# Row sums and inverse deviations of a graph layer's joint stage move to a PSUM bank of their own, and the transposed weighted rows of two edge groups share one bank

## What the reference computes

```
h = relu(layernorm(x))                       # each row on its own: mean and variance over 64 features
score = sum(h[src] * h[dst]); a = softmax of score over the edges with one dst
out = segment_sum((h @ W_conv + b)[src] * a, dst) + relu(h @ W_res + b)
x = x + batchnorm(out)                       # mean and variance over all 100000 rows
h2 = relu(layernorm(x))
x = h2 + gelu(gelu([h2, boxes] @ W_c1 + b) @ W_c2 + b), plus x
    where boxes = segment_sum(gelu(gelu([h2[dst'], h2[src'], edge] @ W_m1) @ W_m2), index)
```

## Time and profile before

| what | value |
|---|---|
| time, median of three runs (range) | 1961.68 us (1946.9 to 1965.65) |
| span of the profiled execution, first to last instruction | 1753.3 us |
| median of the runs less that span | 208.4 us |
| PE busy / DVE busy / ACT busy / POOL busy | 1375.6 / 1361.7 / 833.2 / 1363.7 us |
| mean granted TensorE clock | 0.831 |

### The profile page before, as it was taken

The page is one execution under the profiler, slowest core; times in us unless marked ns, Lnnn a source line. Parts: engine busy times, 40 slices in busy tenths (PEclk is TensorE's granted clock), DMA queues, the critical chain, the costliest instruction groups (busy, mean ns, idle before and its releaser), DMA issues.

```text
span 1753.3 us, 21724 instructions
## 1 busy us (share of the span) xinstructions
PE 1375.6 (78%) x6521; PEld 942.1 (54%) x6521; DVE 1361.7 (78%) x2229; ACT 833.2 (48%) x1448; POOL 1363.7 (78%) x1135
## 2 busy tenths in 40 slices
PE   3487777777776776988999889858889988787993
PEld 1266666666555564766667666634445444343541
DVE  8899899989877858898889888825767766555871
ACT  4655455545543435776668666621333432332441
POOL 7777777778777778788888887675767768888676
PEclk9788889888887877898889888955888987886987
DMA  7788776545543363444545565545656554545520
GB/s 210 249 283 290 282 264 219 165 145 157 161 150 96 106 224 102 157 166 166 201 162 186 174 200 178 160 98 108 121 120 124 118 117 97 107 89 98 122 48 18
DMA packets 154342, 273.55 MB, mean 156 GB/s; under 512 B 58386, under 2 KB 69361, under 8 KB 154228
## 3 DMA queue, kind: packets, MB, share of 16 engines
q1 hardware_dynamic: 71144, 183.91, 31.1%
q0 software_dynamic: 68112, 49.85, 16.7%
q10 hardware_dynamic: 14972, 38.41, 5.9%
HBM read 151.68 MB, written 121.80 MB: 156 GB/s over the span
## 4 chain that ended last, share of the span: by engine, by line
POOL 40%; issue 20%; DVE 18%; PE 13%; DMA 6%; ACT 2%; SPq 0%; POOLq 0%; DVEq 0%; ACTq 0%
POOL agg_rows L591 11%; POOL out L591 10%; POOL agg_ring L587 7%; DVE stat L756 4%; POOL xt L637 3%; DVE stat L764 3%; POOL part L587 3%; DMA rr<-edge_x 3%; DMA edge_agg<-agg_ring 2%; POOL rr L631 2%; DVE xc L770 1%; PE banks L1350 1%; DVE sums L821 1%; PE banks L1542 1%; PE banks L1540 1%
## 5 line engine op out<-in xcount | busy, mean ns | idle before, releaser
L587 POOL DMA_INDIRECT agg_ring<-agg_rows,edge_idx x196 | 233.2, 1190 | 112.2 <-DMA edge_agg<-agg_ring 57.2
L591 POOL DMA_INDIRECT agg_rows<-agg,put_first x196 | 234.0, 1194 | 55.9 <-issue 54.7
L587 POOL DMA_INDIRECT part<-in_x,edge_idx x192 | 217.3, 1132 | 58.5 <-issue 58.2
L591 POOL DMA_INDIRECT out<-agg,put_last x196 | 212.0, 1082 | 59.6 <-issue 59.6
L1335 PE MATMUL banks<-ident,xc 128*128 128x128 f32 (+1 forms) x784 | 135.1, 322 | 141.6 <-DVE xc L770 140.9
L1466 PEld LDWEIGHTS banks<-packed,cT 97*128 97x128 f32 (+1 forms) x1568 | 210.4, 218 | 45.3 <-issue 44.3
L1466 PE MATMUL banks<-packed,cT 97*128 97x64 f32 (+1 forms) x1568 | 218.6, 303 | 0.5 <-ACT cT L1198 0.5
L1335 PEld LDWEIGHTS banks<-ident,xc 128*128 128x128 f32 (+1 forms) x784 | 113.3, 177 | 152.0 <-DVE xc L770 130.8
L1456 PE MATMUL banks<-hT,packed 64*96 64x512 f32 (+1 forms) x392 | 125.5, 718 | 47.6 <-ACT cT L1198 43.0
L1081 ACT ACTIVATE hT<-banks 128x512 f32<-128x512 f32 (+1 forms) x98 | 55.4, 595 | 205.7 <-PE banks L1335 204.3
L587 POOL DMA_INDIRECT x_ring<-in_x,edge_idx x104 | 121.4, 1167 | 34.2 <-issue 34.2
(11 more groups left out here) (163 smaller groups left out, 3351.2 us busy)
## 6 DMA issues: line engine op xcount, KB each, us to landing
xt<-in_x SPq DMA_DIRECT2D x84, 512.0 KB, 5.2
r_rows<-rT ACTq DMA_DIRECT2D x48, 512.0 KB, 5.4
agg_rows<-rb SPq DMA_DIRECT2D x48, 512.0 KB
out<-xt SPq DMA_DIRECT2D x36, 512.0 KB, 3.0
edge_r<-rr ACTq DMA_DIRECT2D x48, 256.0 KB, 5.0
rT<-r_rows SPq DMA_DIRECT2D x24, 512.0 KB, 6.5
part<-r_rows SPq DMA_DIRECT2D x24, 512.0 KB, 6.9
rr<-edge_r SPq DMA_DIRECT2D x48, 256.0 KB, 3.2
```

Of the source, the lines that this page charges most:

```text
L587: A.indirect_dma_start(to, None, table[:, :], bass.IndirectOffsetOnAxis(ap=idx, axis=0), bounds_check=limit, oob_is_err=False).then_inc(si ...
L591: A.indirect_dma_start(table[:, :], bass.IndirectOffsetOnAxis(ap=idx, axis=0), rows_of, None, bounds_check=limit, oob_is_err=False).then_i ...
```

## The change

Bank 5 of PSUM becomes `row_stat`. The row sums of `center` and `edge_center` are written there by L764, and L766 reads them there. The last instruction of the inverse deviations (L702) writes its result there instead of to `stat`, and `relu_scale` (L770) reads it there. Since bank 5 is taken, the transposed weighted rows of even and odd groups both go to bank 4: `transpose_weighted(n)` waits for the scan of group n-1 instead of n-2, and TensorE's order changes: only the transposes of a-2 stand at the head of a round, those of b-2 come after `conv_product(a-2)`.

```diff
--- before.py
+++ after.py
@@ -217,6 +217,7 @@
             return W[i // 2][:, (i % 2) * HALF:(i % 2 + 1) * HALF]
 
         bank_sum = bank(3)
+        row_stat = bank(5)
 
         s_w = sem("weights_loaded")
         s_idx = sem("edge_idx_loaded")
@@ -689,7 +690,7 @@
         def _(dve):
             V = nc.vector
 
-            def inverse_sqrt(total, tmp, n_mean, eps, done):
+            def inverse_sqrt(total, tmp, n_mean, eps, done, root=None):
                 v, y, a = tmp
                 done(V.tensor_scalar(v, total, n_mean * SQUEEZE, eps * SQUEEZE, ALU.mult, ALU.add))
                 done(V.tensor_scalar(y.bitcast(I32), v.bitcast(I32), -0.5, MAGIC, ALU.mult, ALU.add))
@@ -699,7 +700,8 @@
                 done(V.tensor_tensor(a, y, y, ALU.mult))
                 done(V.tensor_tensor(a, a, v, ALU.mult))
                 done(V.scalar_tensor_tensor(out=a, in0=a, scalar=-CUBIC1, in1=a, op0=ALU.add, op1=ALU.mult))
-                done(V.scalar_tensor_tensor(out=y, in0=a, scalar=CUBIC0, in1=y, op0=ALU.add, op1=ALU.mult))
+                done(V.scalar_tensor_tensor(out=y if root is None else root, in0=a, scalar=CUBIC0, in1=y, op0=ALU.add,
+                                            op1=ALU.mult))
 
             def in_stage(st, step):
                 k = [0]
@@ -777,6 +779,12 @@
                 return stat[0:p, i, 2 * R + (g % 2) * ER:2 * R + (g % 2 + 1) * ER]
 
 
+            def node_stat(i, s, p):
+                return row_stat[0:p, i * P + (s % 2) * R:i * P + (s % 2 + 1) * R]
+
+            def edge_stat(i, n, p):
+                return row_stat[0:p, i * P + 2 * R + (n % 2) * ER:i * P + 2 * R + (n % 2 + 1) * ER]
+
             dve.wait_ge(s_m, 1)
 
             def center(s):
@@ -784,19 +792,19 @@
                 dve.wait_ge(A_x.of(s), A_x.after(s))
                 A_t.done(dve, s - CS)
                 A_sq.done(dve, s - 2)
-                subtract_mean(xc[s % CS][0:p, :], xt[s % XS][0:p, :], dstat(0, s, p), A_ctr, s, 1)
+                subtract_mean(xc[s % CS][0:p, :], xt[s % XS][0:p, :], node_stat(0, s, p), A_ctr, s, 1)
 
             def edge_center(n):
                 p = edges_of(group_of(n))
                 dve.wait_ge(G_x.of(n), G_x.after(n))
                 E_t.done(dve, n - 4)
                 E_w.done(dve, n - 4)
-                subtract_mean(ec[n % 4][0:p, :], x_ring[n % GS][0:p, :], estat(0, n, p), E_ctr, n, 1)
+                subtract_mean(ec[n % 4][0:p, :], x_ring[n % GS][0:p, :], edge_stat(0, n, p), E_ctr, n, 1)
 
             def edge_score(n):
                 p = edges_of(group_of(n))
                 t_ = ec[n % 4][0:p, :]
-                relu_scale(rows(t_), rows(t_), estat(3, n, p), E_h)
+                relu_scale(rows(t_), rows(t_), edge_stat(1, n, p), E_h)
                 dve.wait_ge(E_h.sem, E_h.after(n))
                 E_sc.done(dve, n - 1)
                 V.tensor_tensor(rows(prod[0:p, :]), side(t_, 0), side(t_, 1), ALU.mult).then_inc(E_sc.sem, 1)
@@ -819,7 +827,7 @@
                 E_scan.done(dve, n - 1)
                 carry = sums[1 - n % 2][:, 0:1] if n else 0.0
                 V.tensor_tensor_scan(sums[n % 2][:, 0:c][:, ::-1], same[n % 2][0:D + 1, 0:c][:, ::-1],
-                                     bank(4 + n % 2)[0:D + 1, 0:c][:, ::-1], carry,
+                                     bank(4)[0:D + 1, 0:c][:, ::-1], carry,
                                      ALU.mult, ALU.add).then_inc(E_scan.sem, 1)
 
             def edge_finish(n):
@@ -839,7 +847,7 @@
                 A_ss.done(dve, last_step)
                 E_ss.done(dve, last_edge)
                 inverse_sqrt(stat[:, 1, c0:c1], tuple(stat[:, i, c0:c1] for i in (2, 3, 4)), 1.0 / D, LN_EPS,
-                             in_stage(N_inv, t_))
+                             in_stage(N_inv, t_), row_stat[:, P + c0:P + c1])
 
             for t_ in range(ROUNDS):
                 steps = node_pair(t_)
@@ -872,7 +880,7 @@
                     if s is not None:
                         p = nodes_of(s)
                         h_ = rows(xc[s % CS][0:p, :])
-                        relu_scale(h_, h_, dstat(3, s, p), A_h)
+                        relu_scale(h_, h_, node_stat(1, s, p), A_h)
                     if is_group(n):
                         edge_score(n)
                     if is_group(n - 2):
@@ -1353,9 +1361,9 @@
             def transpose_weighted(n):
                 p = edges_of(group_of(n))
                 pe.wait_ge(E_w.sem, E_w.after(n))
-                E_scan.done(pe, n - 2)
+                E_scan.done(pe, n - 1)
                 for j in range(EJ):
-                    ins = T.transpose(bank(4 + n % 2)[0:D + 1, j:p * EJ:EJ], weighted[n % 2][0:p, j, :],
+                    ins = T.transpose(bank(4)[0:D + 1, j:p * EJ:EJ], weighted[n % 2][0:p, j, :],
                                       ident[0:p, 0:p])
                 ins.then_inc(E_wt.sem, 1)
 
@@ -1403,9 +1411,8 @@
             for t_ in range(ROUNDS):
                 steps = node_pair(t_)
                 edges = edge_pair(t_)
-                for n in edges:
-                    if is_group(n - 2):
-                        transpose_weighted(n - 2)
+                if is_group(edges[0] - 2):
+                    transpose_weighted(edges[0] - 2)
                 for n in edges:
                     if is_group(n - 4):
                         edge_stats(n - 4)
@@ -1420,6 +1427,8 @@
                         edge_r_product(n)
                     if is_group(n - 2):
                         conv_product(n - 2)
+                    if n == edges[0] and is_group(n - 1):
+                        transpose_weighted(n - 1)
 
 
             pe.wait_ge(s_bnd, BN_PARTS)
```

## The result

The changed kernel takes 2089.68 us (median of four runs, 2074.5 to 2100.1), the kernel before, run beside it, 1954.29 us (1942.1 to 1965.7): ratio 1.066, 95% interval 1.057 to 1.074. That is 135 us slower, where 43 us were forecast, and outside the range. The sign and the place were right; the size was not, and the trace from which it was worked out turned out not to be one of the timed executions.

What follows compares the result with a forecast made beforehand. VectorE was taken to bound the joint stage, then late gathers. New wait 74.1, gather waits -28.9, node stage -1.9 and PSUM operands 0 gave +43.3 us, from 1961.7 to 2005.0 us; range 1986 to 2038.

Steps and rivals of the forecast that it cites:

- The sign and the place: Slower by over 1% (chance 0.92), through a new VectorE wait before each round's second scan.
- the sum: Whole kernel: new wait 74.1, gather waits -28.9, node stage -1.9, PSUM operands 0, together +43.3 us.
- The new wait: Joint stage, second scan of a round: VectorE waits for TensorE's late transposes, mean 3.50 us per full round, 74.1 in all.
- The waits for gathers: Joint stage, row sums from group 37 on: five VectorE waits for gathered rows disappear, -28.9 us.
- much slower: Rival, TensorE's chain: clock stays low to its end, 2077 us, about 2040 in half the rounds; chance 0.14.
- The operands in PSUM: VectorE's 13 instructions per full round using the new bank: -1.6 to +4.6 us by the rows, taken as 0.
- The 21 us: Same VectorE instructions: estimate from the skill page's 65 ns more per PSUM access, not adopted in the forecast.
- The port rival: GpSimd's gathers shorten, order doesn't count: 1930.9 us, if the new wait is under 1.3 us per round; chance 0.03.
- No change: Rival, TensorE's chain: clock stays high, each full round waits only 1.24 us, 1962.1 us (+0.4); chance 0.05.

Runs made afterwards that it cites:

- e6: Kernel before the change, unedited, run again with its own profile: 1740.4 us.
- e16: Kernel before the change, unedited, run later for its trace: 1970.9 us, one execution.
- e5: Changed kernel, unedited, beside the kernel before: 1777.3 us against 1740.8, ratio 1.021.
- e7: Changed kernel, unedited, once more: 1792.2 us in a single execution, beside 1745.5 for the kernel before.
- e17: Changed kernel, unedited, run later for its trace: 2076.5 us, one execution.
- e1: Kernel before with only TensorE's new order; sums and deviations stay in SBUF, a bank for each group parity: 1782.27 us against 1741.24, ratio 1.024.
- e3: Changed kernel with the transposes of b-2 moved up, right behind the transposes of group a: 1724.51 us, ratio 0.990 to the kernel before.
- e4: Kernel before with the transposes of b-2 at e3's early place; sums and deviations in SBUF, separate banks: 1743.92 us, ratio 1.001.
- e11: Kernel before with 64 added transposes in front of the first step's transposes in each round: 1873.3 us.
- e12: Changed kernel with the same 64 added transposes per round as e11: 1957.5 us.
- e18: Same kernel as e3, unedited, run later for its trace: 2022.7 us, one execution.
- e15: Kernel before with TensorE's idle time before the first step's transposes filled by 24 identity transposes: 1996.2 us, beside 1962.4 without.

## Why the prediction was wrong, point by point

**The failed step** is the last of the sum: "The profiled span of 1753.3 would become 1796.6; with the 208.4 us that lie between span and median in the table, unchanged, 1961.7 + 43.3 = 2005.0 us." The spans lie only about 2 us under their times. The 208.4 us were the difference between an execution of the first level and timed runs of the second, and they lay inside the joint stage, in waits of VectorE (231.6 of the 235 us between e6 and e16), largely behind the engine whose chain was being priced. The sum priced the first level: +43.3, measured +36.5 (e5) and +46.7 (e7, one execution). At the second level two of its terms are wrong. The new wait, 74.1 us, measured 295.1 us (226.5 + 68.6). The waits for gathers, -28.9 us, aren't there to be saved: e16 has none. The kernel before has other waits there, 287.7 us in all (e16), and a part of them goes when the new wait comes: the changed kernel has 387.6 us in all (e17). The difference, +99.9 us, is nearly the whole of the +105.6 us between these two executions.

**The new wait.** Right in place and mechanism: e1 alone 82.3 us, e5 78.6, and e3 takes it away. The chain was sized from a trace of the first level. The rival "much slower" (2040 to 2077, chance 0.14) asked for TensorE's clock to stay at its lower level to the end of the chain. That came true in half of the rounds: in the changed kernel's first profile the conv product of group a-2 runs at 0.50 from start to end in 12 of 25 rounds, in the profile of before and in e5 in none. Its price was about right as well (2.4 us of work more in the round shown above, where it had 2.8). But the same chain is 5.1 us longer by idle time, behind signals of TensorE that come late, and for this no rival had a place. So the rival is the nearest to the measured 2089.7 us in part by luck. Whether the low clock comes from the idle time, or both from one cause, stays open.

**The gathers.** Their waits are gone, as forecast, in e5 and in e1. In e1 82.3 us of new waits cost 41 us; 28.9 of the other 41 would be these waits, and for the remaining 12 no run names a place. At the second level the kernel before has no such waits, and the term is nothing.

**The operands in PSUM.** At 0 ns for VectorE the term held: 682 and 691 ns against 676 and 692. The 21 us by the Trainium skill, page "VectorE: DVE Perf Modes", section on the TRN2 errata, did not appear. The port rival was half true: the gathers got shorter, and once the new wait is taken out the kernel with the operands in PSUM is 19 us faster (e3 against e4). The shorter gathers are as the Trainium skill, page "SBUF — State Buffer", section "Who interferes with whom", would have it. The rival lost against the order, by the condition given for it: a new wait of under 1.3 us per round, where 3.3 were measured.

**No change.** The clock would have had to stay high in the chain; it did not (1.97 us for the eight transposes above, as in the earlier trace rows).

**What of the 135 us is shown.** 36 to 47 us are the order at the first level. The delay by hand shows that a late TensorE costs the changed order more, up to 84 us, since the old one has room. The rest was seen and not explained: at the second level ScalarE's copies start late for 290 us in the changed kernel and for 143 us in the kernel before (e17, e16), and the chain runs more often at the lower clock. The second level gave +106 us in e17 against e16 and +135 us in the first comparison, so its size is known to some 30 us only. Why TensorE's signals come late there, and why more often in the changed kernel, stays open.

## What to carry to other kernels

Before pricing a change, put the profiled span beside the time of its own execution; if only a median of other runs is given and it is far from the span, the trace may be of another condition, and the missing time can sit in the chain that the change touches. A step moved behind a chain costs that chain's lateness as well as its length: of TensorE's first delay the old order passed on 46 to 51 us, the changed one 81 to 96. An idle time without a named cause is best checked against the end of what the program makes it wait for. And split a change that does two things: at the first level the PSUM operands, shared bank included, were a gain of 19 us, the late place of four transposes a loss of 53 (e5 against e3), and only the place had to differ.

## What the runs showed of the hardware that was not expected

- The same kernel took 1741 us at some times and 1962 us at others, with all executions made together at one level. The whole difference was in one stage. The record numbers the chips, and chip 6 stands beside both: 1741.0 us with e11 and e12, 1965.9 us with e16 half an hour later. So the number of the chip doesn't settle the level.
- At the second level what follows TensorE starts late by up to 14 us, and once in each of e16, e17 and e18 by 38 to 49 us, after TensorE's work has ended by the record; at the first level never by over 0.32 us. In e15 TensorE is also seen to stop between matmuls that wait for nothing: in the rows above they start 0.73 to 2.10 us apart, with the granted clock at 0.54 over the stretch and DMA at a share of 0.26:

```profile
553.00:569.40 16.40, 5.51 (x15) 2.68 (x15) 10.79 (x14) 0.00 (x0) 12.94 (x12) 0.54 0.26 69
```

At the lower clock level the transposes of one step start every 0.25 us (1.97 us for eight); these intervals are 3 to 8 times as long. Whether this is the same thing as the late starts is not shown.
- A wait of TensorE under "issue" need not be a stop of its own: 213 of 235 us in e17 end with the copy or scaling that was waited for. The first level has no wait of ScalarE or VectorE under "remote", the second has 69 to 241 us of VectorE's (e17, e18) and 290 to 393 us of ScalarE's (e16, e17).
